# The order of work at the head of a three-layer kernel: the first expert unit directly behind the first transposes

## The reference

```python
def ffn(x):                                  # 2048 x 128
    logits = flat @ Wr + br                  # 8 experts
    probs = softmax(logits); vals, idx = top_k(probs, 2)
    w = vals / (sum(vals) + 1e-9)
    for e in range(8):
        we = sum(w * (idx == e))
        hmid = gelu(flat @ W1[e] + b1[e])    # 128 -> 512
        out_acc += we[:, None] * (hmid @ W2[e] + b2[e])
        weight_acc += we
    return out_acc / (weight_acc + 1e-9)
x = x + 0.5 * ffn(layernorm(x))
x = x + attention(layernorm(x))              # 16 heads, key 16, value 64, softmax over the query axis
x = x + 0.5 * ffn(layernorm(x))
```

## Time and profile before

| | |
|---|---|
| median of 3 runs | 820.52 us (819.36 to 821.1) |
| profiled execution, its own time | 819.94 us |
| its span | 818.1 us |
| PE busy | 780.2 us (95%) |
| DVE busy | 677.1 us (83%) |
| ACT busy | 617.4 us (75%) |
| Pool busy | 202.8 us (25%) |
| mean granted clock of PE | 0.989 |

### The profile page before, as it was taken

How to read it: one execution, slowest core, us unless ns; L and a number is a source line. 1 busy time by engine, 2 the same in 40 slices (tenths; PEclk the granted TensorE clock), 3 DMA queues, 4 the chain that set the end, 5 groups by cost and what they waited for, 6 DMA issues and landing times.

```text
span 818.1 us, 11781 instructions
## 1 busy us (share of the span) xinstructions
PE 780.2 (95%) x3626; PEld 464.3 (57%) x3626; DVE 677.1 (83%) x1353; ACT 617.4 (75%) x1018; POOL 202.8 (25%) x263
## 2 busy tenths in 40 slices
PE   7999999998948999999999999999999999999996
PEld 5778888886724333333333333333349678888885
DVE  7778888878727999999999888888875878888886
ACT  4867777765725999999998888888864767777762
POOL 3116532334200111111111111211121117333322
PEclk8999999999988999999999999999999999999999
DMA  5041213110798111111311110011000042202111
GB/s 171 1 158 51 104 52 103 53 52 0 276 328 322 51 52 52 52 52 52 104 52 52 52 44 24 36 52 52 1 2 1 4 155 94 99 20 97 52 51 52
DMA packets 29509, 63.04 MB, mean 77 GB/s; under 512 B 5264, under 2 KB 10768, under 8 KB 27408
## 3 DMA queue, kind: packets, MB, share of 16 engines
q1 hardware_dynamic: 29456, 62.39, 21.7%
HBM read 44.42 MB, written 17.96 MB: 76 GB/s over the span
## 4 chain that ended last, share of the span: by engine, by line
PE 82%; DVE 6%; DMA 5%; SPq 3%; ACT 2%; issue 1%; POOL 1%; POOLq 0%; DVEq 0%; ACTq 0%
PE ps L910 29%; PE ps L896 10%; PE ps L358 6%; PE ps L359 6%; PE ps L360 6%; PE ps L370 6%; PE ps L369 6%; PE ps L371 6%; PE ps L917 4%; SPq L823 2%; DMA w2raw<-in_w 2%; DMA qk_parts<-stlo 2%; DVE hlo L625 2%; POOL acc L481 1%; DVE hhi L621 1%
## 5 line engine op out<-in xcount | busy, mean ns | idle before, releaser
L1067 DVE TENSOR_SCALAR_CACHE_REDUCE ef<-ps 128x1024 f32<-128x1024 f32 x256 | 308.5, 1215 | 22.8 <-PE ps L896 15.4
L1002 ACT ACTIVATE ef<-ef,nmax 128x1024 f32<-128x1024 f32 x256 | 294.4, 1150 | 26.9 <-DVE ef L1067 19.5
L910 PE MATMUL ps<-ef,vs 128*64 128x512 f32 x1024 | 249.5, 605 | 3.9 <-DVE xt L1085 3.8
L435 ACT ACTIVATE ps<-ps,b_sb 128x512 f32<-128x512 f32 x256 | 169.1, 663 | 102.5 <-PE ps L360 100.5
L625 DVE TENSOR_TENSOR hlo<-ps,hhi 128x512 fp32r<-128x512 f32 x256 | 165.5, 686 | 4.8 <-ACT ps L435 0.7
L1113 POOL TENSOR_TENSOR vs<-V,rsum 128x128 f32<-128x128 f32 x128 | 51.4, 401 | 332.8 <-DVE rsum L1073 332.8
L910 PEld LDWEIGHTS ps<-ef,vs 128*64 128x64 f32 x1024 | 62.1, 136 | 120.7 <-issue 109.4
L621 DVE CAST hhi<-ps 128x512 fp32r<-128x512 f32 x128 | 87.6, 685 | 50.0 <-ACT ps L435 50.0
L481 POOL TENSOR_TENSOR acc<-acc,ysc 128x512 f32<-128x512 f32 x56 | 72.0, 1289 | 155.4 <-DVE ysc L648 154.8
L358 PE MATMUL ps<-xhi,w1lo 128*128 128x512 f32 x256 | 103.4, 404 | 3.5 <-DVE hlo L625 3.5
L359 PE MATMUL ps<-xlo,w1hi 128*128 128x512 f32 x256 | 101.8, 398 | 0.0
(11 more groups left out here) (95 smaller groups left out, 675.3 us busy)
## 6 DMA issues: line engine op xcount, KB each, us to landing
gb<-gates SPq DMA_DIRECT2D x16, 1024.0 KB, 4.6
qk_parts<-sthi SPq DMA_DIRECT2D x32, 256.0 KB, 3.6
qk_parts<-stlo SPq DMA_DIRECT2D x32, 256.0 KB, 3.9
qs<-qk_parts SPq DMA_DIRECT2D x16, 512.0 KB, 4.2
ks<-qk_parts SPq DMA_DIRECT2D x16, 512.0 KB, 5.2
w1raw<-in_w SPq DMA_DIRECT2D x16, 256.0 KB, 5.1
w2raw<-in_w SPq DMA_DIRECT2D x16, 256.0 KB, 5.5
xt<-in_x SPq DMA_DIRECT2D x4, 256.0 KB, 4.5
```

Source lines behind the costliest of these rows:

```text
L435: nc.scalar.activation(bank(mc), bank(mc), ACT.Gelu, bias=b1_sb[:, u, mc:mc + 1]).then_inc(F.gelu, 1)
L910: last = nc.tensor.matmul(bank(6 + half)[x * VD:(x + 1) * VD, :], vs[:, t % VRING, x * VD:(x + 1) * VD], ef[:, (2 * t + x) % ERING, half * ...
L1002: nc.scalar.activation(ef[:, c, :], ef[:, c, :], ACT.Exp, scale=-1.0, bias=nmax[:, c:c + 1], accum_out=esum[:, c:c + 1]).then_inc(s_exp, 1)
L1067: nc.vector.tensor_scalar(ef[:, c, :], bank(slot_bank(u), 2), -1.0, None, ALU.mult, ALU.min, accum_out=nmax[:, c:c + 1]).then_inc(s_max, 1)
```

## The change

Only the head of the first layer changes.

- SP: the identity gets a semaphore of its own, `s_id`; the first-layer weights of expert 0 are issued ahead of x of group 1; the bias of unit 0 comes ahead of the second-layer weights.
- ACT and Pool split the first-layer and the second-layer weights of the first expert each on its own semaphore, in both feed-forward layers; Pool does `rstd` of group 1 between the two parts and that of group 2 behind them.
- PE: four transposes, `hidden(0,0)`, then the transposes of group 1, its wait for the router's weights, the logits of group 0, `hidden(0,1)`, transposes of group 2, logits of group 1, `output(0,0)`.
- ACT: for groups 0 and 1 `xhi` is written first, and `xf` later (`late_full_act`).
- DVE: the statistics of groups 1 to 3 and the scalings are put elsewhere, `front(0,0)` comes ahead of the low part of group 1.

```diff
@@ -188,12 +189,18 @@
                 last = nc.tensor.transpose(bank(forward_bank(n, g))[:, t * P:(t + 1) * P], xn[:, g % 2, t, :], ident)
             last.then_inc(n.fwd, 1)
 
+        def full_act(act, n, g):
+            nc.scalar.activation(xf[:, g * 512:(g + 1) * 512], bank(forward_bank(n, g)), ACT.Copy).then_inc(n.x32, 1)
+
         def high_act(act, n, g):
-            cols = slice(g * 512, (g + 1) * 512)
             act.wait_ge(n.fwd, g + 1)
-            if n.k != 1:
-                nc.scalar.activation(xf[:, cols], bank(forward_bank(n, g)), ACT.Copy).then_inc(n.x32, 1)
-            nc.scalar.activation(xhi[:, cols], bank(forward_bank(n, g)), ACT.Copy).then_inc(n.hi, 1)
+            if n.k == 2 or (n.k == 0 and g >= 2):
+                full_act(act, n, g)
+            nc.scalar.activation(xhi[:, g * 512:(g + 1) * 512], bank(forward_bank(n, g)), ACT.Copy).then_inc(n.hi, 1)
+
+        def late_full_act(act, n, g):
+            act.wait_ge(n.lo, g + 1)
+            full_act(act, n, g)
 
         def rstd_pool(pool, n, g):
             r = rstd[:, g * TPG:(g + 1) * TPG]
...
@@ -268,9 +278,15 @@
         SKEW = 3
         ACT_HI = 2
 
+        def load_first_layer(q, F, e, u):
+            q.dma_start(w1raw[:, u, :], w1[bass.ds(e, 1), :, :].rearrange("a p n -> (a p) n")).then_inc(F.w1[u], 16)
+
+        def load_second_layer(q, F, e, u):
+            q.dma_start(w2raw[:, u, :], w2[bass.ds(e, 1), :, :].rearrange("a p n -> (a p) n")).then_inc(F.w2[u], 16)
+
         def load_expert(q, F, e, u):
-            q.dma_start(w1raw[:, u, :], w1[bass.ds(e, 1), :, :].rearrange("a p n -> (a p) n")).then_inc(F.w[u], 16)
-            q.dma_start(w2raw[:, u, :], w2[bass.ds(e, 1), :, :].rearrange("a p n -> (a p) n")).then_inc(F.w[u], 16)
+            load_first_layer(q, F, e, u)
+            load_second_layer(q, F, e, u)
 
         def load_gates(q, F, e, u):
             src = gd[F.f].rearrange("a b -> (a b)").rearrange("(e n) -> e n", e=E)[bass.ds(e, 1), :]
...
@@ -285,12 +301,20 @@
                 load_bias(sp, F, e, e)
 
         def first_weights_act(act, F):
-            act.wait_ge(F.w[0], 32)
-            high_weights(F, 0)
+            act.wait_ge(F.w1[0], 16)
+            nc.scalar.activation(w1hi[:, 0, :], w1raw[:, 0, :], ACT.Copy).then_inc(F.w1hi, 1)
+            act.wait_ge(F.w2[0], 16)
+            nc.scalar.activation(w2hi[:, 0, :], w2raw[:, 0, :], ACT.Copy).then_inc(F.whi, 1)
 
         def first_weights_pool(pool, F):
+            pool.wait_ge(F.w1hi, 1)
+            nc.gpsimd.tensor_tensor(w1lo[:, 0, :], w1raw[:, 0, :], w1hi[:, 0, :].bitcast(F32),
+                                    ALU.subtract).then_inc(F.w1lo, 1)
+            if F.f == 0:
+                rstd_pool(pool, norms[0], 1)
             pool.wait_ge(F.whi, 1)
-            low_weights(F, 0)
+            nc.gpsimd.tensor_tensor(w2lo[:, 0, :], w2raw[:, 0, :], w2hi[:, 0, :].bitcast(F32),
+                                    ALU.subtract).then_inc(F.wready, 1)
 
         def high_weights(F, u):
             nc.scalar.activation(w1hi[:, u, :], w1raw[:, u, :], ACT.Copy)
...
@@ -346,7 +370,9 @@
 
             def hidden(i, s):
                 u, tt = (s // GR) % 2, s % GR
-                if tt == 0:
+                if isinstance(i, int) and i == 0 and s == 0:
+                    pe.wait_ge(F.w1lo, 1)
+                elif tt == 0:
                     pe.wait_ge(F.wready, i * 2 + (s // GR + 1))
                 if isinstance(i, int) and i == 0 and s < GR:
                     pe.wait_ge(n.lo, tt + 1)
...
@@ -361,6 +387,8 @@
 
             def output(i, s):
                 u = s // GR
+                if isinstance(i, int) and i == 0 and s == 0:
+                    pe.wait_ge(F.wready, 1)
                 pe.wait_ge(F.scaled, i * 8 + (s + S0 - 3))
                 y = bank(Y_BANKS[s % 4])
                 for mc in range(MC):
...
@@ -372,20 +400,27 @@
                 last.then_inc(F.y, 1)
 
             def first():
-                forward_pe(pe, n, 0)
-                forward_pe(pe, n, 1)
                 if outproj:
+                    forward_pe(pe, n, 0)
+                    forward_pe(pe, n, 1)
                     outproj(2)
-                logits_pe(pe, F, 0)
-                logits_pe(pe, F, 1)
-                hidden(0, 0)
-                if outproj:
+                    logits_pe(pe, F, 0)
+                    logits_pe(pe, F, 1)
+                    hidden(0, 0)
                     pe.wait_ge(n.res, 1)
                     outproj(3)
-                forward_pe(pe, n, 2)
-                hidden(0, 1)
-                if outproj:
+                    forward_pe(pe, n, 2)
+                    hidden(0, 1)
                     pe.wait_ge(n.res, 2)
+                else:
+                    forward_pe(pe, n, 0)
+                    hidden(0, 0)
+                    forward_pe(pe, n, 1)
+                    pe.wait_ge(s_cst, 48)
+                    logits_pe(pe, F, 0)
+                    hidden(0, 1)
+                    forward_pe(pe, n, 2)
+                    logits_pe(pe, F, 1)
                 output(0, 0)
                 forward_pe(pe, n, 3)
                 logits_pe(pe, F, 2)
...
@@ -439,16 +474,26 @@
                 if s % GR == 0:
                     u = (s // GR + 1) % 2
                     act.wait_ge(F.y, i * 8 + (s + Y0))
-                    act.wait_ge(F.w[u], (i + (s // GR + 1) // 2) * 32 + 32)
+                    act.wait_ge(F.w1[u], (i + (s // GR + 1) // 2) * 16 + 16)
+                    act.wait_ge(F.w2[u], (i + (s // GR + 1) // 2) * 16 + 16)
                     high_weights(F, u)
 
             def first():
                 high_act(act, n, 0)
-                high_act(act, n, 1)
-                front(0, 0)
-                high_act(act, n, 2)
-                front(0, 1)
-                back(0, 0)
+                if n.k == 0:
+                    front(0, 0)
+                    high_act(act, n, 1)
+                    late_full_act(act, n, 0)
+                    front(0, 1)
+                    late_full_act(act, n, 1)
+                    high_act(act, n, 2)
+                    back(0, 0)
+                else:
+                    high_act(act, n, 1)
+                    front(0, 0)
+                    high_act(act, n, 2)
+                    front(0, 1)
+                    back(0, 0)
                 high_act(act, n, 3)
                 front(0, 2)
                 act.wait_ge(F.sh, 1)
...
@@ -652,18 +697,19 @@
             def first():
                 if n.k == 0:
                     statistics_dve(dve, n, 0)
+                    scaled_dve(dve, n, 0)
                     statistics_dve(dve, n, 1)
-                    scaled_dve(dve, n, 0)
+                    low_dve(dve, n, 0)
+                    scaled_dve(dve, n, 1)
                     statistics_dve(dve, n, 2)
-                    scaled_dve(dve, n, 1)
-                    low_dve(dve, n, 0)
-                    statistics_dve(dve, n, 3)
+                    front(0, 0)
                     low_dve(dve, n, 1)
                     scaled_dve(dve, n, 2)
+                    statistics_dve(dve, n, 3)
+                    front(0, 1)
+                    low_dve(dve, n, 2)
                     scaled_dve(dve, n, 3)
-                    dve.wait_ge(s_cst, 64)
-                    front(0, 0)
-                    low_dve(dve, n, 2)
+                    dve.wait_ge(s_cst, 48)
                 else:
                     scaled_dve(dve, n, 0)
                     scaled_dve(dve, n, 1)
...
@@ -1124,15 +1170,16 @@
                 sp.dma_start(xt[:, g * TPG:(g + 1) * TPG, :], x_v[g]).then_inc(s_x[g], 16)
 
             load_x(0)
-            sp.dma_start(consts[:, :], cst).then_inc(s_cst, 16)
+            sp.dma_start(consts[:, :], cst).then_inc(s_id, 16)
+            load_first_layer(sp, ffns[0], 0, 0)
             load_x(1)
-            load_expert(sp, ffns[0], 0, 0)
+            load_bias(sp, ffns[0], 0, 0)
+            load_second_layer(sp, ffns[0], 0, 0)
             load_x(2)
             load_x(3)
             sp.dma_start(wr_sb[:, :], wr).then_inc(s_cst, 16)
             sp.dma_start(br_sb[:, :], br.unsqueeze(0).broadcast_to([P, E])).then_inc(s_cst, 16)
             sp.dma_start(b2_sb[:, :], b2).then_inc(s_cst, 16)
-            load_bias(sp, ffns[0], 0, 0)
             load_expert(sp, ffns[0], 1, 1)
             load_bias(sp, ffns[0], 1, 1)
             att_weights_sync(sp)
...
@@ -1150,9 +1197,9 @@
         def _(pool):
             nc.gpsimd.memset(mhalf[:, :], -0.5).then_inc(s_fill, 1)
             pool.wait_ge(s_fill, 1)
-            for g in range(3):
-                rstd_pool(pool, norms[0], g)
+            rstd_pool(pool, norms[0], 0)
             first_weights_pool(pool, ffns[0])
+            rstd_pool(pool, norms[0], 2)
             rstd_pool(pool, norms[0], 3)
             ffn_pool(pool, ffns[0])
             for g in range(1, GR):
...
@@ -1185,7 +1232,7 @@
             pe.wait_ge(s_warm, 1)
             for _ in range(WARM):
```

(7 more changed lines are left out.)

3 lines of the change are left out of this document (2 added, 1 removed).

## The result

The changed kernel takes 827.57 us (median of 5 runs, 825.64 to 829.55) against 820.52 for the kernel before (5 runs): ratio 1.009, interval 1.0065 to 1.0114. Its profiled execution took 825.88 us with a span of 824.1, 6.0 more than the span before. The forecast was 821.8 and its range ended at 824.8.

What follows compares the result with a forecast made beforehand. The head's chain on PE up to output(0,0), which releases logits and router, was taken as the bound. Its start moved from 22.09 to 23.4, so 819.94 + 1.3 = 821.2, median 821.8 us; range 820.4 to 824.8.

Steps and rivals of the forecast that it cites:

- The order: Head of the first layer: rearranged work starts output(0,0) at 23.4 instead of 22.09 us, logits of group 1 standing ahead.
- the sum: Head timeline added from profile rows: hidden(0,0) at 9.7 to 9.9, hidden(0,1) at 17.3, output(0,0) at 23.4 us.
- the +1.3: At the start of output(0,0): 23.4 - 22.09 = +1.3 us, passed on to the router, gates and end.
- Scaling 1.12: DVE in the head: the scaling of group 1 takes 1.12 us, with no hold-up from Pool.
- Rival 2: Head: hidden(0,0) cold (+2.4, 822.9), or one 1.27 us Pool operation between two DVE scalings (+2.5, 823.0); chance 0.14.
- Forecast (+1.3, clock held): Main case: head 1.3 us later with PE's clock staying up, median 821.8 us; chance 0.48.
- I take hidden(0,0) as warm: First unit on PE: 2.9 us without 512-column matmuls before it, shorter than both earlier cases, so full clock.
- rival 1: Clock falls before hidden(0,1): +1.87, sum +3.2, 823.7 us; with output(0,0) slow too, 2.0 more, 825.7; chance 0.27.
- Rival 3: At 237 to 251 us the clock might not fall, giving back up to 2.0 us: -0.7, 819.8; chance 0.07.
- Rival 4: A hole behind the router takes up the 1.3 us, so the end hardly moves: 820.5; chance 0.04.
- The router's shift is the shift of the end.: From router to end: the router's delay, 31.3 instead of 29.99 us, passes unchanged through gates and reload.

Runs made afterwards that it cites:

- changed_again: The changed kernel once more, unedited, with no edit against it; 826.54 us, 1.0076 of the kernel before.
- pool_waits: Against the changed kernel, Pool's low parts of the first weights wait until the scalings of groups 0, 1 and 3 are done; 826.81 us, 1.0076 of before.
- xf_early_pool_waits: Against the changed kernel, ACT's full copies ahead of the Gelus and Pool's low parts waiting for the scalings; 822.83 us, 1.0029 of before.
- xf_early: Against the changed kernel, ACT makes the full copies of groups 0 and 1 ahead of the Gelus of units 0 and 1; 827.99 us, 1.0085 of before.
- before_router_late: Against the kernel before, eight chained memsets on DVE between the last logits and the router; 826.86 us, 1.0076 of before.

## Why the prediction was wrong

- **The order.** Borne out as far as the runs go. With the locks away `hidden(0,0)` and `hidden(0,1)` started where the sum had them (9.90, 17.17), and the way from a warm `hidden(0,1)` to `output(0,0)` was 6.25 us for 6.1. Together they give the +1.3, from two runs.
- **"Scaling 1.12", the step that failed first.** The sum priced every scaling at 1.1 because the rows showed none slowed by Pool's `pow`. But that operation is 128x4; no row had a 512-wide one beside a scaling, the text said so, and still gave this case a small chance. Measured: 2.18, 2.06 and 3.08. The Trainium skill, page "SBUF — State Buffer", section "Who interferes with whom", was right on the 512-wide operations, and this case's traces agree in both directions, 1.11 without the neighbour and 2.05 to 2.21 with it, 3.04 to 3.08 beside two. In the sum it meant +1.0 at `hidden(0,0)`.
- **The second and the third meeting.** Rival 2 counted one, `w1lo` beside the scaling of group 0. Its own times had the other: `w2lo` behind the second `rstd`, from 10.4, and the scaling of group 1 from 10.4 as well. Both together put `hidden(0,1)` some 1.7 us behind the sum, not 1.3. The third was not seen at all: `scaled_dve(3)` was moved behind `front(0,1)`, and there it meets both of Pool's low parts of expert 1. It was priced at 1.1 and said to be done when PE wants it; it ended at 29.04, PE waited 0.78, and the way to `hidden(0,2)` grew by 1.1. So in the first profile the locks are some 2.8 of the 4.3 us at the gate copy. That the engines "meet only at semaphores", as the introduction has it, is the same error in words.
- **"Forecast (+1.3, clock held)", the step that failed second.** No trace of the changed kernel had the whole head at full clock. "I take hidden(0,0) as warm" was wrong in the first profile and cost next to nothing there; what cost was the clock behind it. In `changed_again` and `pool_waits` the first unit was warm and the second unit and `output(0,0)` cold, as in rival 1, for 1.87 us on the first of these legs in `changed_again`. To compare a hole with two falls (5.0 and 3.7 us) and call the shorter one safe was no bound: in the first profile PE idled only 0.83 and 1.50 us, with four transposes in between, and the clock fell in the second of these holes; the longest idle time before or around a fall in the second unit was 2.43 in `changed_again`, 2.44 in `pool_waits`, 2.87 in `xf_early_pool_waits` and 3.87 in `xf_early`.
- **The range.** Rivals 1 and 2 were priced each by itself, 823.7 and 823.0, and the range left out that they come together. By the prediction's own terms, 821.8 + 1.9 and 2.0 for a cold second unit and output + 1.2 for one lock = 826.9, against 827.6 measured, and that without the two meetings that it left out. That it comes so close is partly chance, since the clock differs from execution to execution.
- **Rival 3** (not slower, by a clock that holds at 237 to 251 us) didn't happen. The granted clock fell there in all 13 profiles, with means of 0.66 to 0.80 in 237 to 262 us. **Rival 4** fell with `before_router_late`.
- **"The router's shift is the shift of the end."** Not quite. From the router's first operation to the gate copy nothing was lost, but the end moved 6.0 us for 4.3. Over the 13 profiles, of 12 kernels, the time from the gate copy to the end of the span is 774.3 to 777.3 us, and the profile that the forecast was built on is the one at the lower end.
- A small slip, without effect: two copies of 0.60 behind 14.5 and the logits of 0.81 end at 16.5, and not at 16.3; DVE's 17.3 is later all the same.

## What to carry to other kernels

When a change moves a wide Pool operation or a DVE operation, list for each pair what stands beside what afterwards, at every place that moves, and price an unseen pair by what is known of its kind and not by the nearest row of another size. Finding one such pair is a reason to look for the next: here there were three. Holes of two microseconds on PE in a sparse part are not paid once: each can cost the half clock of the unit behind it, so sum them together and put the sum in the range. An order edit that shows nothing may be covered by a second bottleneck at the same place; try the two together before dropping either.
